# The first FFN of batch 1 beside the attention of batch 0 in a two-FFN transformer layer on one core

## The chip, the core and the metric

The kernel runs on 1 core of one Trainium2 chip. The engines of the core are PE (TensorE, matrix products and transposes), DVE (VectorE), ACT (ScalarE), POOL (GpSimd) and SP (SyncE, which here only issues DMAs). Each runs its own stream of instructions in order; they meet at semaphores. The metric is the time of one execution in microseconds (us), as the median of several.

## What is computed

The reference applies one block to x, 8 batches of 512 rows and 512 columns in f32:

```python
x = x + 0.5 * ffn(layernorm(x))           # gate, up: 512 -> 2048, silu(gate) * up, down: 2048 -> 512
x = x + attn(layernorm(x))                # 16 heads of 32; unit-norm q and k, rope on every other head,
                                          # times q_gain, causal softmax, times w_out
x = x + 0.5 * ffn(layernorm(x))           # the same FFN weights
```

The batches don't depend on each other. Inside a batch the three lines follow one another.

## The kernel before

All weights are loaded once, scaled and split into two f16 parts (high and low) that stay in SBUF. Every product is three f16 matmuls (high x high, high x low, low x high; the helper `three`, L826 to L828), each with its own weight load.

The work of a batch has three parts. I call them FFN1, attention and FFN2.

- An **FFN** takes 32 steps (`STEPS`): 2 halves of 256 rows by 16 chunks of 128 hidden columns. A step, or chunk, is `gate` (12 matmuls of 128x256), `up` (12 more), `gated` (tanh on ACT at L548, two products on DVE at L688 and L690), `parts` (high part on ACT at L553, low part on DVE at L694) and `down` (6 matmuls of 128x512 into PSUM bank 0 and 1, or 6 and 7). After the last down of a half, `residual` (L700 on DVE) adds the sum to x. The downs run two steps behind the gates.
- A **layer norm** has 4 row tiles. For each: `stats` (L661 to L665 on DVE, a power on POOL at L413), `norm` (L675 on DVE), `turn` (4 transposes on PE, L871), `split` (high part on ACT at L495, low part on DVE at L683). In the names (name, u, t) u is the norm: 0 of FFN1, 1 of attention, 2 and 3 of FFN2 (tiles 0 and 1, tiles 2 and 3 of the next passage).
- **Attention** has two halves of 8 heads: `qkv` products (WQ), q and k normalised and rotated (`unit`; L418 and L432 to L437 on POOL), transposed (`stack turn`, L932 and L936), row maxima of the scores (L738 on DVE), scores (L980), `exp` (L533, L537 on ACT, L759 on DVE), `values` (L993, L994), and at the end the product with w_out and `out residual` (L783 on DVE), which writes the result x2 of attention.

Two buffers of 512 x 512 hold x: xa takes the input and FFN1's sum, xb takes x2 and FFN2's sum, and SP stores xb. SP loads the next x into xa when x2 is done.

The order is written out by one function, `order(fill)`, a list of named stages; every engine goes through the same list and runs the stages it has. `stream(fill)` gives the FFN steps in their order, `ffn_units` makes of step j a unit of three pieces (down of step j - 2, gate, up), and inside attention the calls of `some()` put one piece or more between its stages. Pieces left over at the end stand ahead of the product with w_out (`o += sum(pieces, [])`). There are three forms:

- `batch(0, 0, False)`: FFN1 of batch 0, then its attention with nothing in between; the last of the weights are prepared beside its FFN1.
- a loop of B - 1 = 7 passages of `batch(it, 1, True)`: FFN1 of batch it + 1 (behind two steps of FFN2 of batch it), then attention of batch it + 1 with the rest of FFN2 of batch it between its stages.
- `batch(0, B, None)`: FFN2 of batch 7.

Of the kernel before, what the change touches and what calls it, by code (L numbers as in the profile page):

```python
# [49 lines left out]
def build(nc, x, w_qkv, w_out, q_gain, w_gate, w_up, w_down, rope, out):  # L50
# [30 lines left out]
    xb = words("xb").rearrange("p (t d) -> p t d", t=TT)  # L81

# [104 lines left out]
    def per_step(wait, fill):  # L187


        place_of = {fi: j for j, fi in enumerate(stream(fill))}  # L190

        def step(name, f, i, back=0):
            j = place_of[f, i] - back
            if fill is not False:
                wait(name, 2 * STEPS, j + 1 - STEPS)
            elif j >= 0:
                wait(name, 2 * STEPS, j + 1)
        return step

# [28 lines left out]
    def order(fill):  # L228
# [4 lines left out]
        if fill is None:  # L233
# [9 lines left out]
        if fill:  # L243
            (g0, u0), (a0, g1, u1), (d0, g2, u2) = (units.pop(0) for _ in range(3))
            o += [("norm", 3, 2), ("stats", 0, 0)] + g0 + [("turn", 3, 2), ("norm", 3, 3), ("stats", 0, 1), ("split", 3, 2)]
            o += u0 + [("turn", 3, 3), ("norm", 0, 0), ("split", 3, 3)] + a0 + g1
            o += [("turn", 0, 0), ("norm", 0, 1), ("split", 0, 0)] + u1
            o += [("turn", 0, 1)] + d0 + [("split", 0, 1)] + g2 + u2
# [9 lines left out]
        if not fill:  # L258
# [3 lines left out]
        for i in range(STEPS + 2):  # L262
# [13 lines left out]
        for hf in range(2):  # L276
            turns = []
            for t in range(TT + 1):
# [21 lines left out]
                if fill or t == TT:  # L300
                    o += turns
                    turns = []
# [45 lines left out]
    with nc.Block() as block:  # L348

        @block.sync  # L350
        def _(sp):
# [18 lines left out]
            with sp.Fori(0, B - 1) as it:  # L370
                for th in range(2):
                    sp.wait_ge(s["x2_done"], it * TT + 2 * th + 2)
                    sp.dma_start(xa[:, 2 * th:2 * th + 2, :], half_of(x[it + 1], th)).then_inc(s[f"x_in{th}"], 16)
                for th in range(2):
                    sp.wait_ge(s["out_ready"], it * TT + 2 * th + 2)
                    sp.dma_start(half_of(out[it], th), xb[:, 2 * th:2 * th + 2, :]).then_inc(s[f"stored{th}"], 16)
            for th in range(2):
                sp.wait_ge(s["out_ready"], (B - 1) * TT + 2 * th + 2)
                sp.dma_start(half_of(out[B - 1], th), xb[:, 2 * th:2 * th + 2, :]).then_inc(s[f"stored{th}"], 16)
# [4 lines left out]
        def _(pool):  # L384
# [22 lines left out]
            def batch(it, ahead, fill):  # L407
# [3 lines left out]
                def stats(u, t):  # L411
                    wait("var_ready", 12, 4 * u + t + 1)
# [47 lines left out]
            batch(0, 0, False)  # L460
            with pool.Fori(0, B - 1) as it:
                batch(it, 1, True)

        @block.scalar
        def _(act):
# [20 lines left out]
            def batch(it, ahead, fill):  # L486
# [3 lines left out]
                def split(u, t):  # L490
                    if u < 3:
                        wait("xt_ps", 12, 4 * u + t + 1)
                    else:
                        wait("xt_ps", 12, 8 + t + 1, -1)
                    nc.scalar.activation(XT[u // 2][:, 0, :, t * P:(t + 1) * P], ps(turn_bank(u, t)).rearrange("p (k n) -> p k n", k=KC), ACT.Copy).then_inc(s["xt_hi"], 1)  # L495
# [72 lines left out]
            batch(0, 0, False)  # L568
            with act.Fori(0, B - 1) as it:
                batch(it, 1, True)  # L570
            batch(0, B, None)

        @block.vector
        def _(dve):
# [68 lines left out]
            def batch(it, ahead, fill):  # L643
                wait = per(dve, it, ahead)
                step = per_step(wait, fill)
                n = [0]
# [6 lines left out]

                def stats(u, t):
                    src = (xa, xa, xb)[u]
                    if u == 0:
# [6 lines left out]
                    V_.memset(carrier[:, 4 * u + t:4 * u + t + 1], 0.0)  # L663
# [3 lines left out]
                def norm(u, t):  # L667
                    src = (xa, xa, xb, xb)[u]
                    k, batch = (4 * u + t, 0) if u < 3 else (8 + t, -1)
                    wait("rstd_ready", 12, k + 1, batch)  # L670
                    if k >= 2 or fill is not False:
                        wait("xt_ps", 12, k - 1, batch)
# [4 lines left out]
                def split(u, t):  # L677
                    if u < 3:
                        wait("xt_hi", 12, 4 * u + t + 1)
                    else:  # L680
                        wait("xt_hi", 12, 8 + t + 1, -1)
                    c = slice(t * P, (t + 1) * P)
                    V_.tensor_tensor(XT[u // 2][:, 1, :, c], ps(turn_bank(u, t)).rearrange("p (k n) -> p k n", k=KC), XT[u // 2][:, 0, :, c], ALU.subtract).then_inc(s["xt_lo"], 1)  # L683
# [12 lines left out]
                def residual(f, th):  # L696
                    step("down_done", f, HC * (th + 1) - 1)
                    dst, name = ((xa, "x1_done"), (xb, "out_ready"))[f]
                    for t in (2 * th, 2 * th + 1):
                        V_.scalar_tensor_tensor(out=dst[:, t, :], in0=ps(6 * f + t % 2), scalar=unscale[:, 0:1], in1=dst[:, t, :],  # L700
# [78 lines left out]
                def out_residual(_, t):  # L779
                    wait("op_ps", TT, t + 1)  # L780
                    if t % 2 == 0 and fill:
                        wait(f"stored{t // 2}", 16, 16, -1)
                    V_.scalar_tensor_tensor(out=xb[:, t, :], in0=ps(t % 3), scalar=unscale[:, 2:3], in1=xa[:, t, :], op0=ALU.mult, op1=ALU.add).then_inc(s["x2_done"], 1)  # L783
# [29 lines left out]
                assert fill is None or n[0] == LINKS, (n[0], LINKS)  # L813

            batch(0, 0, False)
# [248 lines left out]
```

## Time and profile before

| | us |
|---|---|
| median of 3 runs | 3144.57 |
| lowest, highest | 3142.15, 3144.73 |
| span of the profiled execution | 3141.4 |
| PE busy in it | 2873.6 (91%) |
| DVE busy | 1808.9 (58%) |
| ACT busy | 1225.9 (39%) |
| POOL busy | 401.2 (13%) |

The span runs from the first to the last instruction of the profiled execution; it is 3.2 us shorter than the median of the runs. The page cuts it into 40 slices with a digit for each engine's busy share and one for the clock that TensorE was granted, in tenths of 2.4 GHz. The timeline gives each instruction's start and duration, and in brackets how long its engine had been idle and who ended that. Matmuls overlap in the pipeline, so the pitch from one start to the next, not the duration, is what one costs.

### The profile page before, as it was taken

What the parts mean: (1) busy time and instruction counts of PE and PEld (TensorE: products, weight loads), DVE (VectorE), ACT (ScalarE), POOL (GpSimd) and SP (SyncE); (2) the same over time, 40 slices, a digit from 0 to 9 for tenths busy, and PEclk for the clock granted to TensorE, in tenths of its full rate; (3) what the DMA queues carried; (4) which work ended last, traced back from release to release, by engine and by line L of the source; (5) the groups of instructions that cost most, each with busy time, mean ns of one, the idle gap of its engine ahead of it and who ended that gap; (6) DMA issues with size and microseconds to landing.
All of it is one profiled execution on the core that took longest, in us unless ns stands there. A gap on an engine that the chain in (4) does not pass through costs nothing.

```text
span 3141.4 us, 60646 instructions
## 1 busy us (share of the span) xinstructions
PE 2873.6 (91%) x23744; PEld 2078.2 (66%) x23744; DVE 1808.9 (58%) x4252; ACT 1225.9 (39%) x2218; POOL 401.2 (13%) x438
## 2 busy tenths in 40 slices
PE   4796679999999989999899998999899998999999
PEld 3573357766676667766577666766677665776666
DVE  8645463477535674476634775356744766347743
ACT  5223442355223542255423552235422554235522
POOL 0102200211002200022002110022000220021100
PEclk8896679999999999999999999999999999999999
DMA  6000000000000000000000000000000000000000
GB/s 229 1 1 1 1 14 1 1 8 2 22 1 1 8 22 1 1 2 8 22 1 1 8 2 22 1 1 8 22 1 1 2 8 22 1 1 8 2 8 14
DMA packets 15546, 37.94 MB, mean 12 GB/s; under 512 B 1408, under 2 KB 1408, under 8 KB 14720
## 3 DMA queue, kind: packets, MB, share of 16 engines
q1 hardware_dynamic: 15232, 33.70, 3.0%
q8 instruction: 204, 3.34, 0.4%
q14 instruction: 110, 0.90, 0.1%
HBM read 25.31 MB, written 8.39 MB: 11 GB/s over the span
## 4 chain that ended last, share of the span: by engine, by line
PE 60%; issue 22%; DVE 9%; ACT 5%; POOL 3%; DMA 0%; DVEq 0%; ACTq 0%; POOLq 0%; SPq 0%
PE psum L826 18%; PE psum L827 18%; PE psum L828 18%; ACT arena L537 2%; DVE mneg L738 1%; PE psum L980 1%; ACT arena L533 1%; PE psum L871 1%; PE psum L932 1%; PE psum L936 1%; DVE arena L759 1%; DVE arena L683 1%; POOL rn L418 1%; DVE arena L718 1%; POOL arena L437 1%
## 5 line engine op out<-in xcount | busy, mean ns | idle before, releaser
L826 PE MATMUL psum<-arena,WG 128*128 128x256 f16 x2048 | 564.2, 275 | 25.5 <-issue 19.7
L827 PE MATMUL psum<-arena,WG 128*128 128x256 f16 x2048 | 564.2, 275 | 0.0
L828 PE MATMUL psum<-arena,WG 128*128 128x256 f16 x2048 | 564.1, 275 | 0.0
L826 PE MATMUL psum<-arena,WU 128*128 128x256 f16 x2048 | 561.1, 274 | 0.0
L827 PE MATMUL psum<-arena,WU 128*128 128x256 f16 x2048 | 561.1, 274 | 0.0
L828 PE MATMUL psum<-arena,WU 128*128 128x256 f16 x2048 | 561.0, 274 | 0.0
L688 DVE SCALAR_TENSOR_TENSOR arena<-arena,psum 128x256 f32<-128x256 f32 x512 | 213.7, 417 | 551.9 <-ACT arena L548 551.4
L548 ACT ACTIVATE arena<-psum,tscale 128x256 f32<-128x256 f32 x512 | 242.5, 474 | 670.0 <-PE psum L828 669.4
L826 PE MATMUL psum<-WD,arena 128*128 128x512 f16 x1024 | 389.4, 380 | 34.5 <-DVE arena L694 34.3
L828 PE MATMUL psum<-WD,arena 128*128 128x512 f16 x1024 | 388.6, 379 | 0.0
L827 PE MATMUL psum<-WD,arena 128*128 128x512 f16 x1024 | 388.6, 379 | 0.0
L553 ACT ACTIVATE arena<-arena 128x256 f16<-128x256 f32 x512 | 213.3, 417 | 432.3 <-DVE arena L690 431.5
L694 DVE TENSOR_TENSOR arena<-arena 128x256 f16<-128x256 f32 x512 | 220.2, 430 | 179.9 <-ACT arena L553 179.4
L413 POOL TENSOR_TENSOR rstd<-var,mhalf 128x1 f32<-128x1 f32 x96 | 53.6, 558 | 1783.2 <-DVE var L665 1783.2
L533 ACT ACTIVATE arena<-psum,lnbias,hscale 128x512 f32<-128x512 f32 (+1 forms) x256 | 214.1, 880 | 149.0 <-PE psum L981 148.9
L826 PEld LDWEIGHTS psum<-arena,WG 128*128 128x128 f16 x2048 | 202.0, 99 | 93.0 <-issue 28.3
L418 POOL TENSOR_TENSOR rn<-ss,mhalf 128x16 f32<-128x16 f32 x64 | 186.0, 2906 | 587.5 <-DVE ss L707 586.7
L759 DVE TENSOR_TENSOR arena<-arena 128x512 f16<-128x512 f32 (+1 forms) x256 | 210.9, 824 | 80.8 <-ACT arena L537 77.9
L827 PEld LDWEIGHTS psum<-arena,WG 128*128 128x128 f16 x2048 | 202.2, 99 | 59.7 <-issue 0.3
L690 DVE SCALAR_TENSOR_TENSOR arena<-arena,psum 128x256 f32<-128x256 f32 x512 | 215.3, 420 | 17.6
L738 DVE TENSOR_REDUCE mneg<-psum 128x1 f32<-128x512 f32 (+3 forms) x512 | 214.4, 480 | 11.1 <-PE psum L959 11.1
L828 PEld LDWEIGHTS psum<-arena,WG 128*128 128x128 f16 x2048 | 202.4, 99 | 25.5
(143 smaller groups left out, 4749.5 us busy)
## 6 DMA issues: line engine op xcount, KB each, us to landing
arena<-in_L_attn_x SPq DMA_DIRECT2D x16, 512.0 KB, 3.9
out<-arena SPq DMA_DIRECT2D x16, 512.0 KB, 2.8
arena<-in_L_ffn_w_gate SPq DMA_DIRECT2D x4, 1024.0 KB, 9.2
arena<-in_L_ffn_w_up SPq DMA_DIRECT2D x4, 1024.0 KB, 9.3
WD<-in_L_ffn_w_down SPq DMA_DIRECT2D x4, 1024.0 KB, 11.6
arena<-in_L_attn_w_qkv SPq DMA_DIRECT2D x1, 3072.0 KB, 19.5
WQ<-in_L_attn_w_out SPq DMA_DIRECT2D x1, 1024.0 KB, 21.7
ropet<-rope_table SPq DMA_DIRECT2D x1, 128.0 KB, 2.3
```

What stands on the lines that cost most here:

```text
L418: nc.gpsimd.tensor_tensor(rn[:, c], ss2[:, c], mhalf[:, :], ALU.pow).then_inc(s["r_ready"], 1)
L533: nc.scalar.activation(P32[:, c], ps(0, 0, SW)[:, c], ACT.Exp, bias=lnbias[:, 0:1], scale=hscale[:, k:k + 1])
L548: nc.scalar.activation(fH[i % 2], ps(4 + i % 2, 0, TH), ACT.Tanh, scale=tscale[:, i % HC:i % HC + 1]).then_inc(s["tanh_done"], 1)
L553: nc.scalar.activation(HP[i % 2][0], fH[i % 2], ACT.Copy).then_inc(s["h_hi"], 1)
L688: V_.scalar_tensor_tensor(out=fH[i % 2], in0=fH[i % 2], scalar=1.0, in1=g, op0=ALU.add, op1=ALU.mult).then_inc(s["a_done"], 1)
L690: V_.scalar_tensor_tensor(out=fH[i % 2], in0=fH[i % 2], scalar=2.0 ** -50, in1=u, op0=ALU.mult, op1=ALU.mult).then_inc(s["gated"], 1)
L694: V_.tensor_tensor(HP[i % 2][1], fH[i % 2], HP[i % 2][0], ALU.subtract).then_inc(s["h_lo"], 1)
L738: ins = V_.tensor_reduce(mnegv[:, t, h:h + 1], ps(0, QSEG[t], (t + 1) * P), AX_X, ALU.max, negate=True)
L759: V_.tensor_tensor(PLO[:, c], P32[:, c], PHI[:, c], ALU.subtract).then_inc(s["plo_done"], 1)
L826: T_.matmul(o, lhs(0), rhs(0), start=first, stop=False)
L827: T_.matmul(o, lhs(0), rhs(1), start=False, stop=False)
L828: return T_.matmul(o, lhs(1), rhs(0), start=False, stop=last)
```

## The change

A fourth form takes over. `batch(0, 0, "first")` does FFN1 of batch 0 and then its attention, now with FFN1 of batch 1 between the stages (steps (2, i), residual into xb, layer norm `AHEAD_X` = 4 on 4 tiles, put beside chunks 24 to 32 of FFN1 of batch 0). `batch(0, 1, "second")` does the attention of batch 1 with FFN2 of batch 0 and has no FFN1 of its own. The loop starts with batch 2 and has 6 passages of the old order (its list of stages is unchanged, as is that of "last"). The buffers swap roles: from batch 1 on, the input and FFN1's sum stand in xb, x2 and FFN2's sum in xa; batch 0 keeps xa for all. SP loads x of batch 1 early, behind the end of w_down's preparation and the 4th norm of batch 0. The attention of batch 0 also takes the loop's place for `stack turn` (behind the next qkv).

```diff
+    def x1_of(fill):
+        return xa if fill == "first" else xb
...
+    def norm_of(fill, u, t):
+        if fill == "first":
+            return {0: t, 1: 4 + t if t < 2 else 8 + t, AHEAD_X: 6 + t, 2: 12 + t}[u]
+        if fill == "second":
+            return {3: t, 1: 4 + t, 2: 8 + t}[u]
+        return {3: t - 4, 0: t, 1: 4 + t, 2: 8 + t}[u]
...
     def stream(fill):
-        first = [(0, i) for i in range(STEPS)] if fill is not None else []
-        second = [(1, i) for i in range(STEPS)] if fill is not False else []
-        return second[:AHEAD] + first + second[AHEAD:]
+        first, second, ahead = ([(f, i) for i in range(STEPS)] for f in range(3))
+        if fill == "first":
+            return first + ahead
+        if fill == "loop":
+            return second[:AHEAD] + first + second[AHEAD:]
+        return second
...
-        if fill:
+        if fill != "first":
+            v = 0 if fill == "loop" else 1
             (g0, u0), (a0, g1, u1), (d0, g2, u2) = (units.pop(0) for _ in range(3))
-            o += [("norm", 3, 2), ("stats", 0, 0)] + g0 + [("turn", 3, 2), ("norm", 3, 3), ("stats", 0, 1), ("split", 3, 2)]
+            o += [("norm", 3, 2), ("stats", v, 0)] + g0 + [("turn", 3, 2), ("norm", 3, 3), ("stats", v, 1), ("split", 3, 2)]
...
-        if not fill:
+        if fill == "first":
+            for t in range(TT):
+                for j, name in ((0, "stats"), (1, "norm"), (1, "turn"), (2, "split")):
+                    late.setdefault(HC + 8 + 2 * t + j, []).append((name, AHEAD_X, t))
...
-        for i in range(STEPS + 2):
+        for i in range(STEPS + 2 if fill != "second" else 0):
...
-                if fill or t == TT:
-                    o += turns
-                    turns = []
+                o += turns
+                turns = []
...
+            sp.wait_ge(s["wd_lo"], 4)
+            sp.wait_ge(s["xn_done"], TT)
+            for th in range(2):
+                sp.dma_start(xb[:, 2 * th:2 * th + 2, :], half_of(x[1], th)).then_inc(s[f"x_in{th}"], 16)
+            for th in range(2):
+                sp.wait_ge(s["out_ready"], 2 * th + 2)
+                sp.dma_start(half_of(out[0], th), xa[:, 2 * th:2 * th + 2, :]).then_inc(s[f"stored{th}"], 16)
+            with sp.Fori(0, B - 2) as it:
...
-            batch(0, 0, False)
-            with pe.Fori(0, B - 1) as it:
-                batch(it, 1, True)
-            batch(0, B, None)
+            batch(0, 0, "first")
+            batch(0, 1, "second")
+            with pe.Fori(0, B - 2) as it:
+                batch(it, 2, "loop")
+            batch(0, B, "last")
```

Three places where the streams change. In the rows of after the line numbers are 33 or 34 higher: L721, L723 and L727 are the old L688, L690 and L694.

**PE, where batch 0 goes from FFN1 to its first qkv product (WQ).** Before:

```order
L826 MATMUL psum<-WD,arena 128x512
L827 MATMUL psum<-WD,arena 128x512
L828 MATMUL psum<-WD,arena 128x512
L826 MATMUL psum<-WQ,arena 128x512 [waits pro_lo,sel_done,x1_done,xt_lo]
L827 MATMUL psum<-WQ,arena 128x512
L828 MATMUL psum<-WQ,arena 128x512
```

After:

```order
L860 MATMUL psum<-arena,WU 128x256
L861 MATMUL psum<-arena,WU 128x256
L862 MATMUL psum<-arena,WU 128x256
L860 MATMUL psum<-WQ,arena 128x512 [waits pro_lo,sel_done,x1_done,xt_lo]
L861 MATMUL psum<-WQ,arena 128x512
L862 MATMUL psum<-WQ,arena 128x512
```

The last down of FFN1 (WD) stood right ahead of the qkv product that waits for x1_done; now an up product (WU) of chunk 2 of batch 1 does. In all 3 gate and up products and 1 down of batch 1 stand between the two.

**DVE, in the softmax of the first head group of batch 0.** Before:

```order
L759 TENSOR_TENSOR arena<-arena 128x512 [waits phi_done]
L759 TENSOR_TENSOR arena<-arena 128x768 [waits phi_done]
L738 TENSOR_REDUCE mneg<-psum 128x1 [waits s1_ps] x2
L738 TENSOR_REDUCE mneg<-psum 128x1
L738 TENSOR_REDUCE mneg<-psum 128x1 [waits s1_ps]
L769 RECIPROCAL yrec<-psum 128x4 [waits pv_ps]
L770 COPY arena<-psum 128x4x32
L771 TENSOR_TENSOR arena<-psum,arena 128x4x32 [waits dve_chain]
L773 TENSOR_TENSOR arena<-arena,yrec 128x4x32 [waits y_read]
```

After:

```order
L771 TENSOR_REDUCE mneg<-psum 128x1 [waits s1_ps] x2
L771 TENSOR_REDUCE mneg<-psum 128x1
L771 TENSOR_REDUCE mneg<-psum 128x1 [waits s1_ps]
L721 SCALAR_TENSOR_TENSOR arena<-arena,psum 128x256 [waits tanh_done]
L723 SCALAR_TENSOR_TENSOR arena<-arena,psum 128x256 [waits a_done]
L802 RECIPROCAL yrec<-psum 128x4 [waits pv_ps]
L803 COPY arena<-psum 128x4x32
L804 TENSOR_TENSOR arena<-psum,arena 128x4x32 [waits dve_chain]
L806 TENSOR_TENSOR arena<-arena,yrec 128x4x32 [waits y_read]
L792 TENSOR_TENSOR arena<-arena 128x512 [waits phi_done]
L792 TENSOR_TENSOR arena<-arena 128x768 [waits phi_done]
L727 TENSOR_TENSOR arena<-arena 128x256 [waits h_hi]
```

Between row maxima (L738, now L771), values (L769 on, now L802 on) and low parts of the softmax (L759, now L792) stand the gated products and the low part of an FFN chunk.

**DVE, behind the last out residual of batch 0.** Before (the loop begins; L184 are register instructions that work out semaphore values):

```order
L184 REGISTER_ALU [waits rstd_ready]
L675 TENSOR_SCALAR arena<-arena,mv,rstd 128x512 [waits xt_ps]
L184 ISA
L661 BN_STATS stat<-arena 128x6 [waits x_in0]
L184 ISA
L663 MEMSET carrier 128x1 [waits dve_chain]
L664 BN_AGGR mv<-stat 128x2
L184 REGISTER_ALU
L665 TENSOR_SCALAR var2<-mv 128x1 [waits dve_chain]
L184 REGISTER_ALU
```

After (the straight code of "second"):

```order
L711 TENSOR_SCALAR arena<-arena,mv,rstd 128x512 [waits xt_ps,rstd_ready]
L697 BN_STATS stat<-arena 128x6 [waits x1_done]
L699 MEMSET carrier 128x1 [waits dve_chain]
L700 BN_AGGR mv<-stat 128x2
L701 TENSOR_SCALAR var2<-mv 128x1 [waits dve_chain]
L711 TENSOR_SCALAR arena<-arena,mv,rstd 128x512 [waits xt_ps,rstd_ready]
L697 BN_STATS stat<-arena 128x6 [waits x1_done]
L699 MEMSET carrier 128x1 [waits dve_chain]
L700 BN_AGGR mv<-stat 128x2
L701 TENSOR_SCALAR var2<-mv 128x1 [waits dve_chain]
```

Both go from the last norms of FFN2 (L675, now L711) to new statistics. Before these were of the next input (x_in0) for FFN1; now they are of FFN1's sum (x1_done), for attention.

## Rows read from the trace of the kernel before

**Rows 1.** The page, 40 slices of 78.5 us: PE's busy tenths and its granted clock.

```profile
PE   4796679999999989999899998999899998999999
...
PEclk8896679999999999999999999999999999999999
```

**Rows 2.** Timeline of DVE, columns start us, us, what: first or last L783 of a batch.

```profile
436.41 0.75 DVE L783 SCALAR_TENSOR_TENSOR arena<-psum,unscale,arena 128x512 f32<-128x512 f32 x1 [1.27 <-PE psum L828]
...
442.92 0.74 DVE L783 SCALAR_TENSOR_TENSOR arena<-psum,unscale,arena 128x512 f32<-128x512 f32 x1
...
799.17 0.75 DVE L783 SCALAR_TENSOR_TENSOR arena<-psum,unscale,arena 128x512 f32<-128x512 f32 x1 [1.36 <-PE psum L828]
...
805.68 0.74 DVE L783 SCALAR_TENSOR_TENSOR arena<-psum,unscale,arena 128x512 f32<-128x512 f32 x1
...
2998.39 0.75 DVE L783 SCALAR_TENSOR_TENSOR arena<-psum,unscale,arena 128x512 f32<-128x512 f32 x1 [1.36 <-PE psum L828]
```

**Rows 3.** Stretches: us, then PE, PEld, DVE, ACT, POOL busy, PEclk, DMA share, GB/s.

```profile
93.60:237.10 143.50, 133.02 (x976) 97.59 (x976) 78.76 (x142) 37.73 (x73) 13.48 (x8) 0.96 0.00 1
237.10:443.70 206.60, 133.77 (x992) 79.23 (x992) 112.23 (x267) 89.81 (x131) 43.56 (x44) 0.67 0.01 3
290.00:330.00 40.00, 27.32 (x236) 16.19 (x236) 25.33 (x61) 25.76 (x32) 0.00 (x0) 0.50 0.00 1
443.70:590.80 147.10, 144.97 (x1101) 109.14 (x1101) 63.96 (x158) 35.88 (x79) 4.51 (x8) 0.98 0.02 5
590.80:806.40 215.60, 204.00 (x1846) 144.58 (x1844) 149.33 (x358) 110.20 (x189) 43.65 (x44) 1.00 0.03 9
806.40:957.90 151.50, 146.60 (x1102) 110.07 (x1101) 63.97 (x159) 35.87 (x79) 4.39 (x8) 0.96 0.02 5
```

**Rows 4.** Timeline of PE in the shared stage: units of gate, up, down and turn.

```profile
592.18 0.27 PE L826 MATMUL psum<-arena,WG 128*128 128x256 f16 x1
...
594.80 0.38 PE L826 MATMUL psum<-WQ,arena 128*128 128x512 f16 x1
...
599.14 0.38 PE L826 MATMUL psum<-WD,arena 128*128 128x512 f16 x1
...
600.44 0.60 PE L871 MATMUL psum<-ident,arena 128*128 128x128 f32 x4
...
600.87 0.27 PE L826 MATMUL psum<-arena,WG 128*128 128x256 f16 x1
```

**Rows 5.** Timeline of PE, end of FFN1 of batch 0: idle before, and its releaser.

```profile
234.15 0.39 PE L826 MATMUL psum<-WD,arena 128*128 128x512 f16 x1 [1.09 <-DVE arena L694]
...
237.17 0.38 PE L826 MATMUL psum<-WQ,arena 128*128 128x512 f16 x1 [1.55 <-issue]
```

**Rows 6.** Groups of DVE instructions: busy us, mean ns, idle us before and who ended it.

```profile
L694 DVE TENSOR_TENSOR arena<-arena 128x256 f16<-128x256 f32 x512 | 220.2, 430 | 179.9 <-ACT arena L553 179.4
...
L683 DVE TENSOR_TENSOR arena<-psum,arena 128x512 f16<-128x512 f32 x96 | 66.0, 688 | 40.4 <-ACT arena L495 38.3
L661 DVE BATCH_NORM_STATS2 stat<-arena 128x6 f32<-128x512 f32 x96 | 65.9, 686 | 0.3
...
L675 DVE TENSOR_SCALAR arena<-arena,mv,rstd 128x512 f32<-128x512 f32 x96 | 52.1, 543 | 27.0 <-issue 19.3 <-POOL rstd L413 6.3
...
L664 DVE BATCH_NORM_AGGREGATE mv<-stat 128x2 f32<-128x6 f32 x96 | 17.0, 177 | 4.9 <-issue 1.1
```

**Rows 7.** Timeline of DVE: the fourth norm of batch 0.

```profile
105.10 0.54 DVE L675 TENSOR_SCALAR arena<-arena,mv,rstd 128x512 f32<-128x512 f32 x1
```

**Rows 8.** The page's DMA issues: KB each, median us to landing.

```profile
arena<-in_L_attn_x SPq DMA_DIRECT2D x16, 512.0 KB, 3.9
```

**Rows 9.** Timeline of PE after the attention of batch 0.

```profile
445.19 0.39 PE L826 MATMUL psum<-arena,WG 128*128 128x256 f16 x1 [1.42 <-DVE arena L683]
...
455.17 0.66 PE L871 MATMUL psum<-ident,arena 128*128 128x128 f32 x4 [0.51 <-DVE arena L675]
```

**Rows 10.** Timeline of PE after the first loop-back: the first gate of batch 2.

```profile
810.12 0.39 PE L826 MATMUL psum<-arena,WG 128*128 128x256 f16 x1 [3.13 <-issue]
```

More of the change, by code:

```diff
@@ L190, in per_step, with ffn_norm @@
         place_of = {fi: j for j, fi in enumerate(stream(fill))}
+        late = 0 if fill in ("first", "second") else STEPS
         def step(name, f, i, back=0):
             j = place_of[f, i] - back
[L194 to L197, printed above, removed]
-        return step
+            if fill != "first" or j >= 0:
+                wait(name, 2 * STEPS, j + 1 - late)
+        return step
+    AHEAD_X = 4
+    def norm_of(fill, u, t):
[4 more added lines that the diff above has]
+        return {3: t - 4, 0: t, 1: 4 + t, 2: 8 + t}[u]
+    def ffn_norm(f):
+        return {0: 0, 1: 3, 2: AHEAD_X}[f]
     STEPS = 2 * HC
@@ L566, in batch @@
                      "exp": exp, "y turn": y_turn, "gated": gated, "parts": parts}, fill)
-            batch(0, 0, False)
-            with act.Fori(0, B - 1) as it:
-                batch(it, 1, True)
-            batch(0, B, None)
+            batch(0, 0, "first")
+            batch(0, 1, "second")
+            with act.Fori(0, B - 2) as it:
+                batch(it, 2, "loop")
+            batch(0, B, "last")
         @block.vector
@@ L645, in batch @@
                 step = per_step(wait, fill)
-                n = [0]
+                n = [2 * TT if fill == "second" else 0]
                 def link(ins):
@@ L667, in norm @@
                 def norm(u, t):
[L668 to L672, printed above, removed]
+                    src = normed(u)
+                    k = norm_of(fill, u, t)
+                    wait("rstd_ready", 12, k + 1)
+                    if k >= 2 or fill != "first":
+                        wait("xt_ps", 12, k - 1)
                     if t % 2 and u == 2:
@@ L812, in batch @@
                      "maxima": maxima, "max rows": max_rows, "exp": exp, "y out": y_out, "y turn": y_turn, "out residual": out_residual}, fill)
-                assert fill is None or n[0] == LINKS, (n[0], LINKS)
-            batch(0, 0, False)
-            with dve.Fori(0, B - 1) as it:
-                batch(it, 1, True)
-            batch(0, B, None)
+                assert fill == "last" or n[0] == LINKS + 2 * TT * (fill == "first"), (n[0], LINKS)
+            batch(0, 0, "first")
+            batch(0, 1, "second")
+            with dve.Fori(0, B - 2) as it:
+                batch(it, 2, "loop")
+            batch(0, B, "last")
         @block.tensor
@@ L854, in batch @@
                 step = per_step(wait, fill)
-                bank3 = [("xt_lo", 12, 10, -1) if fill is not False else None]
-                bank2 = [None]
+                bank3 = [("xt_lo", 12, norm_of(fill, 3, 1) + 1) if fill != "first" else None]
+                bank2 = [("x2_done", TT, 3, -1) if fill == "second" else None]
                 scored = [None]
@@ L866, in turn @@
                 def turn(u, t):
-                    k, batch = (4 * u + t, 0) if u < 3 else (8 + t, -1)
-                    wait("xn_done", 12, k + 1, batch)
-                    take(bank3 if turn_bank(u, t) == 3 else bank2, "xt_lo", 12, k + 1, batch)
+                    k = norm_of(fill, u, t)
+                    wait("xn_done", 12, k + 1)
+                    take(bank3 if turn_bank(u, t) == 3 else bank2, "xt_lo", 12, k + 1)
                     for kc in range(KC):
@@ L909, in qkv @@
                         wait("phi_done", 32, 2 * HH)
+                    elif fill == "second":
+                        wait("x2_done", TT, TT, -1)
                     else:
                         wait("x1_done", TT, TT)
-                    if fill is False and i == 0:
+                    if fill == "first" and i == 0:
                         wait("pro_lo", 0, 1 + KC)
@@ L1025, in batch @@
                      "out part": out_part, "out": out_product}, fill)
-            batch(0, 0, False)
-            with pe.Fori(0, B - 1) as it:
-                batch(it, 1, True)
-            batch(0, B, None)
+            batch(0, 0, "first")
+            batch(0, 1, "second")
+            with pe.Fori(0, B - 2) as it:
+                batch(it, 2, "loop")
+            batch(0, B, "last")
 _INS = ["L0_attn_x", "L0_attn_w_qkv", "L0_attn_w_out", "L0_attn_q_gain", "L0_ffn_w_gate", "L0_ffn_w_up", "L0_ffn_w_down"]
```

67 lines of the change are left out of this document (32 added, 35 removed).

## Prediction, written before the changed kernel had run

> **What bounds the kernel now.** I read the page's slices first [rows 1]. PE is 90% busy or more in nearly all of the span; the hole is slices 4 to 6, where both PE's busy share and the granted clock fall to 6 or 7 tenths. The last residual instructions of the attentions, L783 on VectorE (DVE), then cut the span into batches [rows 2]: the one at 442.92 ends the attention of batch 0, the one at 805.68 that of batch 1, and each batch after batch 0 repeats a first FFN and an attention that shares PE with the second FFN of the batch before. Busy time by stage [rows 3] says what limits each:
>
> - attention of batch 0, alone: 206.6 us, of which PE computes 133.8 at a mean granted clock of 0.67. In 290 to 330 us that clock is 0.50, the 1.2 GHz level.
> - attention of batch 1, shared with FFN work: 215.6 us, PE 204.0, clock 1.00. That is 9 us more time, and most of an FFN inside it.
> - first FFN of batch 1: 147.1 us, PE 145.0. Nothing but PE work sets it.
>
> So the shared stages are bound by PE, and the lone attention by its chain through ACT, DVE and POOL. Only this stage has room, and there is one of it. Therefore I build the sum from PE's work plus the few holes in it.
>
> **Prices.** In the shared stage gate and up of one chunk run from 592.18 to 594.80, 2.62 us for 24 matmuls; one down runs from 599.14 to 600.44, 1.30 us for 6; one layer norm turn (4 transposes) from 600.44 to 600.87, 0.43 us [rows 4]. A chunk of FFN thus costs 3.92 us, and 32 of them 125.4 us. All at the 2.4 GHz level.
>
> **The change part by part.** I place each moved piece on the new timeline; t is the start of the first qkv product, as the row at 237.17 now [rows 5].
>
> 1. *End of FFN1 of batch 0.* Ahead of the first qkv product the order puts 3 gate/up and 1 down of batch 1, and 4 more turns: 7.86 + 1.30 + 1.72 = 10.88 us. It takes away two holes of PE, the wait of the last down for L694 (1.09) and the 1.55 us before the first qkv product, which waits for the residual, since other work now stands there [rows 5]. Net 8.2 us: t = 237.2 + 8.2 = 245.4. The 4 norms also add 4 sets of statistics, norm and split on DVE, by the means [rows 6] 0.69 for L661, 0.54 for L675, 0.69 for L683 and three small ones at L664's 0.18 or less, 2.5 us a set at most, and a split and a rstd each on ACT and POOL. One set falls on every second chunk, 7.8 us, where DVE has about 1.3 us per chunk of its own (three like L694's 0.43); I count them at nothing. If that cover were gone it would cost 4 x 2.5 = 10 us.
> 2. *x of batch 1* is now loaded by SP after the 4th norm of batch 0 (L675 at 105.10 [rows 7]) and lands about 3.9 us later [rows 8]; its first reader is chunk 24, near 237 - 9 x 3.92 = 202 us. 90 us of slack, no cost. The stores of batch 0 wait for the same residuals as in the loop now.
> 3. *Attention of batch 0* becomes the shared form. From the first qkv (594.80 [rows 4]) to the end of the last L783 (805.68 + 0.74 = 806.42 [rows 2]) batch 1 takes 211.6 us. Between those points the new order holds the same 27 gates and 28 downs among the attention, and behind its last values product 2 more gate/up and 2 more downs than the loop: 5.24 + 2.60. They stand in a bare FFN tail, whose last down waits as at 234.15, 1.09 us [rows 5]. Total 220.5 us. Batch 0's last L783 ends at 245.4 + 220.5 = 465.9 (now 443.66).
> 4. *Start of batch 1*: no FFN1 any more, only 4 gate/up, 2 downs and 4 turns before its first qkv. From 443.66 to 594.80 there are 151.1 us now, with 37, 35 and 8 of them. Taking 33 x 3.92 + 4 x 0.43 = 131.1 away leaves 20.0 us, which keeps the holes and the half clock behind the last L783 (1.42 and 0.51 us, a first WG matmul of 0.39 us [rows 9] where a warm one takes 0.27 [rows 4]).
> 5. *Attention of batch 1*: 211.6 plus 1 gate/up, 1 down and the 1.09 us tail, 216.6 us. Its last L783 ends at 465.9 + 20.0 + 216.6 = 702.5. Now it is 806.4: **103.9 us gone**.
> 6. *The loop* runs 6 times and no longer 7. The first passage takes 362.76 us (436.41 to 799.17), the later ones (2998.39 - 799.17) / 6 = 366.54 [rows 2]. The difference sits in the start: behind a loop-back PE's first gate idles 3.13 us with "issue" as the reason [rows 10], against 1.42 [rows 9]; the stage with FFN1 takes 151.5 us there, against 147.1 [rows 3]. What is lost is one later passage, with one loop-back: **3.8 us gone**. The last passage and the final FFN stay.
>
> Sum: 103.9 + 3.8 = 107.7 us. The profiled span of 3141.4 becomes 3033.7. The median of the runs, 3144.57, stands 3.2 us above that span, so it becomes **3036.9 us**, a ratio of 0.966.
>
> A shorter way gives the same: the 147.1 + 206.6 us of one FFN1 and the lone attention become one attention stage with its share of chunks.
>
> **Bounds of what the trace does not show.** The new start of batch 1 packs into 20 us four statistics, four norms and four splits (10 us by step 1's set), and about 1.3 us of DVE work for each of 4 chunks: 15 of 20 us, where the same norms had 151 us to settle. The other two norms of this layer follow at once, beside the first qkv. Between nothing (in the loop those two follow at the same place) and their full 5 us on the path, I take nothing: the nearest row is the hole of 0.51 us [rows 9], which the 20 us hold already. On the other side the two tails may find their last part ready (-2.2 us), and the start of batch 1, 5.2 us above its 14.8 us of bare PE work, might lose all of that but the 1.5 us from the last L783 to the first gate (-3.7). So -6 to +5, and a scatter of 2.6 us between the runs of before.
>
> **Rivals.**
>
> *The loop-back is not what makes later passages longer.* Then the first passage is short because a lone attention stands before it, a shared one will stand there now, and the 3.8 us stay: 3040.7. For it: the only short passage is also the only one with that neighbour. Against it: PE's extra hole has "issue" for a reason, no other engine. The Trainium skill (Runtime: NRT & Kernel Launch, Instruction fetch mechanics) states that fetch runs ahead in sequence and that a taken branch out of the window costs a stall. By that rule the 3.8 us go, and by the rival they stay; the row at 810.12 [rows 10] agrees with the rule.
>
> *The low clock belongs to the place, not to idleness (slower).* If PE were granted 0.67 in both new stages as in the lone attention now, 432 us of PE work (204 + 8, and 204 + 16) would take 432 x (1/0.67 - 1) = 213 us more: 3037 + 213 = 3250. It decides from a mean clock of 432 / (432 + 107.7) = 0.80 down. Against it: FFN1 of batch 0 comes earlier and has 0.96, and the shared attention has 1.00 [rows 3]; in the lone one the clock is 0.50 just where PE computes 27 of 40 us. The skill (TensorE: Matmul & The Clock Gate, The HAM clock gate) says that the chip halves this clock when the array has been little busy and gives it back under work; the two stages agree.
>
> *DVE becomes the bound where norms and FFN parts crowd.* The 5 us of the new start or step 1's 10 us, each in full: 3042 to 3047. DVE is 149.3 of 215.6 us busy in the shared stage [rows 3], so waits are short, not absent.
>
> *The hiding doesn't take place.* If x of batch 1 came as late as the last L783 of batch 0, its FFN could not run beside that attention, and 3144 stays. The order and the slack in step 2 speak against it.
>
> **How the numbers follow.** Forecast 3036.9: 0.74. No loop-back gain, 3040.7: 0.10. DVE: 0.08. More gain than the bounds: 0.03. Hiding fails: 0.02. Low clock: 0.03. From the lower bound (-6) to the upper end of the DVE rival and the scatter of before the range is 3031 to 3050. It holds the first three cases; with what may be mis-sized inside the forecast I leave 0.2 outside. Faster by over 0.2% (about what a measurement of this kernel can tell from none): 0.95; within: 0.02; slower: 0.03.
>
> **What would show it.** In the profile of after: no lone attention, granted clock 1.00 from 245 to 466 us; PE busy near 212 us there; the first qkv near 245; the last residual of batch 0's attention ending near 466 and of batch 1's near 702; from the one to the other 237 us; first passage of the loop 363, later ones 366.5. I am wrong if a hole of several us stands before a turn or a gate of the new start (DVE), if the tail of 3 chunks waits more than about 1 us, or if the first passage of the loop takes 366.

## The result and the profile after

| | before | after |
|---|---|---|
| median, us | 3143.36 (3141.70 to 3144.73, 4 runs) | 3031.38 (3028.18 to 3032.48, 4 runs) |
| ratio | | 0.9642, 95% interval 0.9628 to 0.9656 |
| span of the profiled execution | 3141.4 | 3029.8 |

The change takes 112.0 us off; 107.7 were forecast. The mechanism came as predicted, but the saving is 4 to 5 us larger than the forecast, and the time lies at the low edge of the range (3031); a second set of runs (e1, 3030.36) lies below it. So this part is about a small error: which terms of the sum were off, and why the lower bound didn't hold them. One execution of e3, 3199.6 us at a granted clock of 0.912 where the ten others of e3 show 0.957 to 0.959, is left out of its ratio.

In the page's slices after the change, the hole of [rows 1] is gone in both rows:

```profile
PE   4799999999999999998999989999899998999999
...
PEclk8899999999999999999999999999999999999999
```

The stretches of after answer to [rows 3]; the columns are the same. They are FFN1 of batch 0, its attention, the new start of batch 1, its attention, and the first FFN1 of the loop:

```profile
92.35:243.50 151.15, 143.19 (x1070) 106.85 (x1071) 90.81 (x176) 41.46 (x81) 15.95 (x13) 0.96 0.02 8
243.50:464.00 220.50, 207.87 (x1876) 147.22 (x1874) 149.42 (x357) 111.42 (x191) 43.63 (x44) 1.00 0.01 1
464.00:482.90 18.90, 16.88 (x125) 13.07 (x125) 13.70 (x39) 5.44 (x11) 3.01 (x5) 0.91 0.00 1
482.90:699.30 216.40, 203.78 (x1846) 144.32 (x1844) 147.86 (x354) 110.43 (x189) 43.62 (x44) 1.00 0.03 9
699.30:845.80 146.50, 143.83 (x1102) 108.50 (x1101) 64.02 (x159) 35.89 (x79) 4.50 (x8) 0.99 0.02 5
```

The attention of batch 0 now holds 208 us of PE work at a granted clock of 1.00, where it held 133.8 at 0.67. In the new start DVE is busy 13.7 of 18.9 us, and PE 16.9. PE's two idle times there are the 1.50 us before its first gate, shown below, and 0.51 us before a turn, the same as in [rows 9]:

```profile
474.60 0.66 PE L905 MATMUL psum<-ident,arena 128*128 128x128 f32 x4 [0.51 <-DVE arena L711]
```

So no queue of norms on DVE holds PE up. The last out residual of each batch (L816, the old L783) answers to [rows 2]. These are batches 0, 1, 2 and 7:

```profile
463.22 0.74 DVE L816 SCALAR_TENSOR_TENSOR arena<-psum,unscale,arena 128x512 f32<-128x512 f32 x1
...
698.57 0.74 DVE L816 SCALAR_TENSOR_TENSOR arena<-psum,unscale,arena 128x512 f32<-128x512 f32 x1
...
1060.68 0.74 DVE L816 SCALAR_TENSOR_TENSOR arena<-psum,unscale,arena 128x512 f32<-128x512 f32 x1
...
2892.40 0.74 DVE L816 SCALAR_TENSOR_TENSOR arena<-psum,unscale,arena 128x512 f32<-128x512 f32 x1
```

The sum laid beside two executions of the changed kernel (the second is the profile of run e1, below) shows where it was short. A stage ends with the last out residual of its batch, or begins with PE's first gate or first qkv product:

| stage, us | forecast | first profile | e1 |
|---|---|---|---|
| up to the first gate | 93.6 | 92.4 | 93.6 |
| FFN1 of batch 0 | 151.8 | 151.2 | 149.7 |
| attention of batch 0 | 220.5 | 220.4 | 220.4 |
| start of batch 1 | 20.0 | 19.0 | 18.7 |
| attention of batch 1 | 216.6 | 216.4 | 216.4 |
| first passage of the loop | 362.8 | 362.1 | 362.0 |
| five later passages | 1832.7 | 1831.7 | 1830.9 |
| rest, FFN2 of batch 7 | 135.8 | 136.7 | 136.9 |
| span | 3033.7 | 3029.8 | 3028.6 |

The two attentions, which are dense PE work at 2.4 GHz and short holes, agree within 0.2 us. All that differs by more lies where the clock changes, or ahead of the first gate, where the weights are prepared. PE behind the attention of batch 0 shows what I had not priced. This is the timeline at the start of batch 1, the answer to [rows 9]:

```profile
465.57 0.27 PE L860 MATMUL psum<-arena,WG 128*128 128x256 f16 x1 [1.50 <-DVE arena L716]
...
466.49 0.42 PE L860 MATMUL psum<-arena,WG 128*128 128x256 f16 x1
...
469.45 0.27 PE L860 MATMUL psum<-arena,WU 128*128 128x256 f16 x1
```

A 128x256 matmul of 0.42 us is one at 1.2 GHz, of 0.27 one at 2.4. The low stretch begins after the first gate has started and ends before 469.45, some 3.4 us. In the kernel before it began with the first gate, at 445.19, and lasted 5.3 us. I measured this stretch behind every attention, from the start of the first slow 128x256 matmul to that of the last: 2.3 to 9.2 us in both kernels, and not the same at the same place of two executions of one kernel.

### The profile page after: what moved, and what is told of

Its sections match the earlier page's. It is cut to its first block, busy times and chain, and to the rows that moved or that the text cites. A ratio compares the mean times of both kernels' runs of the same rounds, so it can differ in the third digit from the quotient of the medians.

```text
span 3029.8 us, 60069 instructions
## 1 busy us (share of the span) xinstructions
PE 2831.6 (93%) x23744; PEld 2061.9 (68%) x23744; DVE 1807.5 (60%) x4252; ACT 1221.4 (40%) x2218; POOL 402.4 (13%) x438
## 4 chain that ended last, share of the span: by engine, by line
PE 60%; issue 20%; DVE 10%; ACT 6%; POOL 3%; DMA 0%; DVEq 0%; ACTq 0%; POOLq 0%; SPq 0%
PE psum L860 18%; PE psum L862 18%; PE psum L861 18%; ACT arena L567 3%; DVE mneg L771 1%; PE psum L905 1%; DVE arena L792 1%; ACT arena L563 1%; PE psum L968 1%; PE psum L972 1%; PE psum L1016 1%; POOL rn L450 1%; DVE arena L727 1%; DVE arena L716 1%; POOL arena L469 1%
## 5 line engine op out<-in xcount | busy, mean ns | idle before, releaser
L721 DVE SCALAR_TENSOR_TENSOR arena<-arena,psum 128x256 f32<-128x256 f32 x512 | 214.0, 418 | 492.8 <-ACT arena L578 492.3
L727 DVE TENSOR_TENSOR arena<-arena 128x256 f16<-128x256 f32 x512 | 220.6, 431 | 169.6 <-ACT arena L583 169.1
L792 DVE TENSOR_TENSOR arena<-arena 128x512 f16<-128x512 f32 (+1 forms) x256 | 211.2, 825 | 84.3 <-ACT arena L567 82.9
L723 DVE SCALAR_TENSOR_TENSOR arena<-arena,psum 128x256 f32<-128x256 f32 x512 | 215.4, 421 | 17.6
L771 DVE TENSOR_REDUCE mneg<-psum 128x1 f32<-128x512 f32 (+3 forms) x512 | 215.0, 483 | 10.6 <-PE psum L995 10.6
```

The lines of the kernel that those rows point to most:

```text
L721: V_.scalar_tensor_tensor(out=fH[i % 2], in0=fH[i % 2], scalar=1.0, in1=g, op0=ALU.add, op1=ALU.mult).then_inc(s["a_done"], 1)
L723: V_.scalar_tensor_tensor(out=fH[i % 2], in0=fH[i % 2], scalar=2.0 ** -50, in1=u, op0=ALU.mult, op1=ALU.mult).then_inc(s["gated"], 1)
L727: V_.tensor_tensor(HP[i % 2][1], fH[i % 2], HP[i % 2][0], ALU.subtract).then_inc(s["h_lo"], 1)
L771: ins = V_.tensor_reduce(mnegv[:, t, h:h + 1], ps(0, QSEG[t], (t + 1) * P), AX_X, ALU.max, negate=True)
L792: V_.tensor_tensor(PLO[:, c], P32[:, c], PHI[:, c], ALU.subtract).then_inc(s["plo_done"], 1)
```

## The experiments

The times are medians, and the interval behind each ratio is the 95% one. Ratios are to the kernel before, whose runs on the same chip gave 3143.31 for e1 to e4, 3144.24 for e5 to e8 and 3145.29 for e9 to e11.

**e1: the changed kernel again.** 

> The changed kernel once more, to see how much of the 5.5 us by which it beat the forecast (3031.4 against 3036.9) repeats, and in which stage. Theory A (sizes): the saving is 110 to 114 us again, and the stages stand as in the first profile: first qkv 151.2 us behind the first gate, attention of batch 0 220.4, start of batch 1 about 19. Theory B (scatter): the saving varies by 2 us or more from chip to chip and run to run, and the first gate's start (92.35 in the first profile, 93.64 in the kernel before) and the stretches of low clock behind each attention move by about 1 us each.

3030.36 us, ratio 0.9639 (0.9626 to 0.9652): 113.0 us less than before. The saving repeats; it isn't a lucky run. Its stages are in the table: the two attentions and the start of batch 1 agree with the first profile within 0.3 us. FFN1 of batch 0 doesn't (149.7 against 151.2; I had expected 151.2), and the first gate began at 93.58, not 92.35. The trace shows why FFN1 differs: its first matmuls run at 1.2 GHz, 14 of them of 128x256 in e1 and 23 in the first profile, and 5 and 10 more follow behind a hole of 6.53 us near 147 us. A slow one is 0.21 us behind the one before it, a fast one 0.11, so 14 slow ones less are the 1.5 us. Both theories hold in part: about 5 us over the forecast are real, 1 to 2 us in several stages are scatter. The runs of e1 to e11 also show how a span stands to its own run: about 2.0 us below it for the kernel before (1.7 to 2.1), 1.75 for the changed one. I had taken 3.2, by pairing a span with the median of other runs. Some 1.4 us of the forecast time was that.

**e2: one passage outside the loop.**

```diff
-            with pe.Fori(0, B - 1) as it:
-                batch(it, 1, True)
+            batch(0, 1, True)
+            with pe.Fori(0, B - 2) as it:
+                batch(it, 2, True)
```

(the same on the other engines). 

> The kernel before with the first passage of its loop written straight behind batch 0, so that the loop runs 6 times; the list of stages is unchanged. Theory A (a taken branch costs the start of a passage): one loop-back less, 3140 - 3.8 = about 3.8 us faster than before, ratio 0.9988; both straight passages are short ones, the passage behind the peeled one (batch 2) also 362 to 363 us. Theory B (the lone attention in front makes the first passage short): no gain, ratio 1.000, and the passage of batch 2 takes 366.5.

3137.39 us, ratio 0.9983 (0.9974 to 0.9992), 5.9 us faster; by the interval 2.5 to 8.2 us, so it shows that a loop-back costs something, not whether it is 3.8 us. The passages of batches 1 and 2 take 361.5 and 363.6 us, the five behind them 365.4 in the mean. The second of the short ones has a shared attention in front of it, so the rival "no loop-back gain" falls. In this profile the lone attention took 211.0 us and not 206.5, at a clock of 0.66: with a low clock for most of its length, that stage scatters by more than the whole effect sought.

**e3: only the place of the stack turns.**

```diff
-                if fill or t == TT:
-                    o += turns
-                    turns = []
+                o += turns
+                turns = []
```

> The kernel before with only the changed place of the stack turns in the attention of batch 0 (behind the next qkv product). Theory A: this part of the change is worth little by itself, within 0.3% (10 us) either way, since the lone attention waits on its chain ACT, DVE, POOL. I take -5 to 0 us, as the four holes of 6.1 us ahead of the last two turns of each half might shrink. Theory B: it is a large part of the gain, 20 us or more.

3144.47 us, ratio 1.0003 (0.9994 to 1.0012). This part of the change shows no worth of its own, in the kernel where the attention stands alone; the interval leaves room for 2 us of gain or 4 of loss. I had left it unpriced, and that was right.

**e4: all of the change but the hiding.**

```diff
-                if len(pieces) > 1:
+                if len(pieces) > 1 and fill != "first":
```

> The changed kernel with the pieces of the first FFN of batch 1 all put behind the attention of batch 0 and none between its stages. Same work, same buffers, same loads. Theory A (the gain is the room under the lone attention): nearly all of it goes, 245 + 206 for the lone attention, 120 for the FFN behind it, 20 and 217 for batch 1, one loop-back less: 3138 to 3146 us, with the granted clock of the attention near 0.67 again. Theory B (the gain comes from the other parts, the swapped buffers, the early load, the straight code): it keeps half of the gain or more, below 3090 us.

3131.4 us, ratio 0.9964 (0.9950 to 0.9978). Of 112 us 12 are left, and 100 are gone: the gain is the work laid into the room of the lone attention. The new kernel's attention of batch 0 and the FFN behind it, as stretches:

```profile
239.50:446.00 206.50, 139.86 (x1050) 83.92 (x1049) 110.88 (x263) 92.28 (x137) 42.68 (x42) 0.68 0.00 1
446.00:565.50 119.50, 116.13 (x857) 83.82 (x856) 44.04 (x102) 25.27 (x56) 1.12 (x2) 1.00 0.00 1
```

From the first qkv product to the last out residual it takes 326.0 us, the 206 + 120 that I had. The cut at 446.00 is placed by that sum; FFN pieces begin at 431.80 already, ahead of the product with w_out, and up to there the mean clock is 0.65, behind it 1.00. The whole came out 7 us below the low end of what I expected: 5.5 us of that is the first qkv product, at 239.5 and not at 245, since the edit also moves a chunk (3.92 us) from ahead of it to behind the attention. 3.8 us of the 12 were expected as the lost loop-back. By the traces, the two batches up to 801.50 end 4.9 us earlier than before, and the six passages behind them take 6.6 us less than the last six in the kernel before. The first of them has no loop-back in front of it; the later five take 365.8 in the mean instead of 366.4, though no work differs in those. That was the first sign that the passages themselves scatter.

**e5: the six passages written out straight.**

```diff
-            with pe.Fori(0, B - 2) as it:
+            for it in range(B - 2):
                 batch(it, 2, "loop")
```

> The changed kernel with its 6 passages written out straight, no loop on the four computing engines (SP keeps its own). Theory A (the taken branch costs): 5 loop-backs less, each 3.8 to 4.2 us: 19 to 21 us faster than the changed kernel, about 3011 us; each passage takes 362 to 363 us. Theory B (the branch costs nothing, or straight code has to be fetched at the same price): within 3 us of the changed kernel, passages of 366.

3008.07 us, ratio 0.9563 (0.9550 to 0.9576), 23 us less than the changed kernel. Three rows of DVE give the passages, those of batches 2, 3 and 7:

```profile
1061.42 0.74 DVE L816 SCALAR_TENSOR_TENSOR arena<-psum,unscale,arena 128x512 f32<-128x512 f32 x1
1423.17 0.74 DVE L816 SCALAR_TENSOR_TENSOR arena<-psum,unscale,arena 128x512 f32<-128x512 f32 x1
...
2870.43 0.74 DVE L816 SCALAR_TENSOR_TENSOR arena<-psum,unscale,arena 128x512 f32<-128x512 f32 x1
```

361.75 us for the first, (2870.43 - 1423.17) / 4 = 361.8 for the rest. Against 366.3 a loop-back costs 4.5 us, not 3.8. Of these 4.5 us 0.3 lie in the attention, which takes 211.3 us in the straight form and 211.6 in the loop; the rest lies in the start of the passage.

**e6: two passages in each turn of the loop** (3 turns, the passages' order unchanged). 

> The changed kernel with two passages in each turn of the loop, 3 turns: 2 loop-backs, not 5. Theory A: 3 x 4 = 12 us faster than the changed kernel, about 3020 us, and passages alternate between 362 and 366. Theory B: within 3 us of it.

3021.93 us, ratio 0.9603 (0.9590 to 0.9617). 9.5 us less for three loop-backs, where 12 were expected and e5 would give 13.5. Passages behind a loop-back take 365.2 and 367.0, the others 362.5 to 363.5: these are longer than the 361.8 of e5, with low stretches of 4.5 to 6.8 us in front of them instead of 3.3 to 3.8.

**e7: the last down's wait covered.**

```diff
-        o += sum(pieces, [])
-        o += [("out part", 0, 1), ("y turn", 1, 1), ...
+        rest = sum(pieces, [])
+        at = max(k for k, x in enumerate(rest) if x[0] == "down")
+        o += rest[:at] + [("out part", 0, 1)] + rest[at:]
+        o += [("y turn", 1, 1), ...
```

> The changed kernel with the first out part of row tile 1 (9 matmuls, about 1.9 us) put ahead of the last down wherever leftover pieces stand behind the attention. It should cover the wait of 1.09 us of the last down in batches 0 and 1; in the loop this down had no such wait. Theory A: about 2.2 us faster than the changed kernel, 3029. Theory B (the wait only moves to the y turn or the product with w_out behind it): no change.

3026.39 us, ratio 0.9623 (0.9610 to 0.9636), 4 to 6 us less and not 2.2. The hole in the changed kernel is this row of PE, 1.09 us as [rows 5] let expect:

```profile
450.23 0.39 PE L860 MATMUL psum<-WD,arena 128*128 128x512 f16 x1 [1.09 <-DVE arena L727]
```

Here the attentions of batches 0 and 1 take 219.1 and 215.1 us, 1.3 less each: 2.6 us. The attentions in the loop take 211.4 us instead of 211.6, some 1.5 us in six. The rest lies in the starts of the passages: the later ones take 365.4 us instead of 366.3, and in the profile three of five have a low stretch of only 2.3 us. e10 tests whether that is a gain or luck.

**e8: PE kept busy in the lone attention of the kernel before.**

```diff
+                def warm(f, i):
+                    for kc in range(KC):
+                        three(ps(4 + i % 2, 0, TH), lambda q: WG[:, q, kc, 0:P],
+                              lambda q: WU[:, q, kc, 0:TH], kc == 0, kc == KC - 1)
```

at every second call of `some()`. 

> The kernel before with 43 groups of 12 matmuls of 128x256 added on PE alone in the attention of batch 0 (two ahead of its first qkv, the others between its stages), into a PSUM bank that nobody reads there; nothing is left out. They are 56 us of PE work at 2.4 GHz. Theory A (the low clock of that attention is the price of an idle PE): the granted clock rises from 0.67 to 0.9 or more, the attention's own matmuls shrink to full-clock durations, and the stage still takes 198 to 214 us. Theory B (the low clock belongs to this place of the program): it stays near 0.67, the added work takes 84 us or more and the stage 240 us or more.

3136.65 us, ratio 0.9973 (0.9962 to 0.9983): 56 us of work more, 7 us of time less. The stretch of that attention:

```profile
237.70:438.20 200.50, 159.82 (x1486) 113.91 (x1484) 112.06 (x264) 88.45 (x131) 43.63 (x44) 0.95 0.01 4
```

The clock rises from 0.67 to 0.95 at the same place of the program, with the same ACT, DVE and POOL work, and the stage takes 200.5 us, not 206.6 (nor 208.6 and 211.0 as in e3 and e2). So the low clock follows PE's idleness, not the place; the slow rival is refuted. It also splits the cost of the lone attention: the chain through ACT, DVE and POOL needs 200 us at most by itself (the added matmuls may hold it up here and there), and the low clock added 6 or more.

**e9: the holes behind every attention filled.** The same group of matmuls, in the changed kernel, twice at the end of each attention:

```diff
-              ("out", 0, 3), ("turn", 2, 1), ("out residual", 0, 3),
+              ("out", 0, 3), ("warm", 0, 0), ("turn", 2, 1), ("warm", 0, 1), ("out residual", 0, 3),
```

> The changed kernel with two groups of 12 matmuls of 128x256 on PE alone at the end of every attention, one ahead of the last turn and one behind it, into a PSUM bank nobody reads there; nothing is left out. They stand in PE's two holes of 2.27 and 1.4 to 1.5 us. Theory A (the stretch of 1.2 GHz behind each attention, 2.5 to 9.4 us long, is the price of these holes, and its changing length is what makes the passages differ by 2 us): the stretches vanish or shrink, every passage loses 1 to 4 us, 8 to 20 us in all, and the passages agree within 0.5 us. Theory B (the stretch has another cause, or the loop-back alone keeps it): passages stay at 365 to 367 or grow by the 0.3 to 2.6 us of added work that the holes don't take.

3023.56 us, ratio 0.9619 (0.9606 to 0.9632): 6 to 8 us less, with 8 x 2.6 us more PE work. PE at the start of batch 1:

```profile
464.58 0.63 PE L905 MATMUL psum<-ident,arena 128*128 128x128 f32 x4 [0.96 <-DVE arena L716]
465.05 0.27 PE L860 MATMUL psum<-WU,WG 128*128 128x256 f16 x1
...
466.71 0.27 PE L860 MATMUL psum<-arena,WG 128*128 128x256 f16 x1 [0.20 <-DVE arena L716]
```

Of the holes of 2.27 and 1.50 us, 0.96 and 0.20 are left; the first gate stands as far behind the attention as without the added matmuls (1.62 us), and every 128x256 matmul stays at 0.27. No low stretch is left but one, of 3.2 us, behind the first loop-back, where PE still idles:

```profile
1066.98 0.28 PE L860 MATMUL psum<-arena,WG 128*128 128x256 f16 x1 [3.59 <-issue]
```

The five later passages now agree: 364.6 to 365.2 us, where the changed kernel had 365.5 to 367.2. So most of the scatter of the passages was the length of the low stretch. What is left of the cost of a loop-back is 3.1 us: the first passage, with no loop-back in front of it, takes 361.9 us and the later ones 365.0. At the other four loop-backs PE idles 1.9 to 3.4 us before the first gate, without a low stretch behind.

**e10: straight and with the covered wait.** 

> The changed kernel with its 6 passages written out straight and the first out part of row tile 1 ahead of the last down of each attention. Theory A (the two savings add): 23 us of the straight form and 3 to 5 us of the covered wait, 3003 us against 3031, passages of 361. Theory B (the covered wait was worth 5 us only by a luckier low clock behind the loop-backs): 3005 to 3008 us.

3007.36 us, ratio 0.9562 (0.9549 to 0.9576), the same as e5 within the intervals. The attentions of batches 0 and 1 keep their 1.3 us each, but the low stretches behind the attentions are now 3.4 to 5.7 us long instead of 3.3 to 3.8, and the passages take 362.1 us instead of 361.8. So the clock takes the gain back, as in Theory B. That is more than luck in one execution: the mean granted clock is 0.982 to 0.983 in all five runs here and 0.985 to 0.986 in all five of e5 (on another chip; the kernel before has 0.957 to 0.959 on both). Of the 4 to 6 us of e7, 4.1 lie in its attentions; whether the rest was a luckier clock is not shown: its five runs have 0.979 to 0.981, those of the changed kernel 0.980 to 0.982.

**e11: e10 and the filled holes.** 

> The same with the two groups of 12 matmuls of the filled holes at the end of every attention. Theory A (holes cost clock): low stretches of 3.4 us, half of it lost, go away, about 1.7 us in each of 8 starts, 10 to 14 us less than without them: 2990 to 2994 us. Theory B: no gain or a loss of up to 2.6 us for each attention, 3003 to 3023 us.

3000.03 us, ratio 0.9539 (0.9526 to 0.9552). 7.3 us less than e10; I had expected 10 to 14, so the mechanism is right and 1.7 us for a start was too much: it is 0.9. The trace shows where part of it goes. With the clock held, PE reaches the turns of the start earlier and waits longer for the norms on DVE (L713 here), 0.93 and 0.78 us, where e10 has one such wait of 0.51:

```profile
1423.23 0.66 PE L907 MATMUL psum<-ident,arena 128*128 128x128 f32 x4 [0.93 <-DVE arena L713]
```

DVE's rows (L818 here) for batches 3 and 7:

```profile
1418.47 0.74 DVE L818 SCALAR_TENSOR_TENSOR arena<-psum,unscale,arena 128x512 f32<-128x512 f32 x1
...
2863.10 0.74 DVE L818 SCALAR_TENSOR_TENSOR arena<-psum,unscale,arena 128x512 f32<-128x512 f32 x1
```

(2863.10 - 1418.47) / 4 = 361.16, and all six passages are equal to 0.05 us; no low stretch stands behind any attention. It is faster than both kernels, by 145 us (the kernel before, on the same chip) and some 31 (the changed one). A variant with real FFN work in the holes, instead of matmuls that nobody reads, was not tried.

## Why the mechanism was right and the size fell short

What failed are terms of the sum, and then its lower bound. Steps 4 and 6 priced stages with a stretch of low clock in them from one execution as if that length were fixed: the start of batch 1 at 20.0 us, measured 19.0 and 18.7, and the loop's first passage at 362.76, measured 362.1. The step from the span to the median (3.2 us, measured 1.75) and the time up to the first gate (93.6, measured 92.4 and 93.6) were taken from one execution too. The 5.5 us between 3036.9 and 3031.4 add up so, by the first profile: 1.2 start-up, 0.6 FFN1 of batch 0, 1.0 start of batch 1, 0.3 the two attentions, 1.7 the passages, less 0.9 for the last FFN, which came out longer; then 1.4 for the step to the median, and the profiled run lies 0.2 above the median.

- **The bound, and the room in one stage**: right. e4 takes the hiding away and 100 of 112 us with it; e3 shows no worth of the new place of the turns.
- **Steps 3 and 5**, the shared attentions: right to 0.2 us, with the same wait of 1.09 us in front of the last down. Counting PE's instructions at their pitch works where PE is dense and its clock constant. The sign "PE busy near 212 us" was wrong by 4 us: the 204.0 of [rows 3] is counted from 590.8, 4 us ahead of the first qkv product, and the stage holds 207.9. The "shorter way" named under the sum is not worked out there and confirms nothing.
- **Step 1**: right within 0.6 us in the first profile and 2 us in e1. The four extra norms on DVE cost nothing that is seen. Step 2, the early load, too: x of batch 1 is issued at 104.33 us, and no wait for it is seen.
- **Step 4 was mis-sized**, 20.0 against 19.0 and 18.7. I had kept "the holes and the half clock" of the one start that the trace showed in that form. Its low stretch was 5.3 us long, the new ones 3.4 and 2.3. At half speed about half of the difference is time lost.
- **Step 6 was mis-sized** in the same way. The first passage of the kernel before has that 5.3 us stretch inside, so 362.76 was no clean price: 361.8 is (e5), and a loop-back costs 4.5 us, not 3.8. By the first profile that is 0.65 us on the first passage and 1.0 on the later five.
- **The last FFN** erred the other way. Taken over unchanged at 135.8 us, it took 136.7 and 136.9, behind low stretches of 4.4 and 4.9 us where the kernel before had 3.2. That part of the errors cancels is luck.
- **The base**: 1.4 us from pairing a span with the median of other runs, and 1.2 us of start-up in the first profile, none in e1: the first gate comes at 92.1 to 94.5 us over all these profiles, whatever the kernel.
- **The bounds** failed with these terms. I built the low end from holes that might close (-6) and took 2.6 us of scatter on the high end only. Eight starts, each with a low stretch of 2.3 to 9.2 us, were in the sum as one draw each. Their own scatter, some 1 us a passage, and the error of the base belonged at both ends; with what is known now, 3027 to 3050 would have held all runs.
- **The rivals**: the low clock as a property of the place is refuted by e8, and by the 1.00 of both new attentions; DVE as the bound by the 0.51 us above, the only wait of PE for a norm in the new start; the missing loop-back gain by e2 and e5; the failed hiding by the result.

## What to carry to other kernels

A stage that runs alone on its latency chain (each engine waiting for the one before), in a kernel whose other stages are bound by PE, is room for PE work. Here it took in most of an FFN for 14 us more of its own time (206.5 to 220.4), and the gain could be priced by counting at PE's pitch. Before a passage is taken as a unit price, split its holes from the clock behind them: take several executions or several passages, and give the term the spread that they show, at both ends. Where a loop turns only a few times over a long body, compare it with the body written out: here each loop-back cost 4.5 us.

## What the runs showed of the hardware that I had not expected

- **More work, less time.** 43 groups of matmuls that nobody reads made the lone attention 6 us shorter (e8), and two groups behind each attention took 7 us off the kernel (e9, and again in e11 against e10), because PE kept its 2.4 GHz level.
- **Short holes were enough to lose the clock.** Idle times of 2.3 and 1.5 us, with one turn of 0.6 us between them, brought a stretch of 1.2 GHz each time; 0.96 and 0.20 us brought none. Behind filled holes, one idle time of 3.59 us at a loop-back brought a stretch and one of 3.38 us at another did not (e9). The stretch lasted 2.3 to 9.4 us over all profiles and differed between executions. The Trainium skill (TensorE: Matmul & The Clock Gate, The HAM clock gate) says that the number of slow matmuls varies from run to run and is not to be fitted; these traces agree.
- **A loop-back** leaves PE idle for 2.6 to 3.8 us before its first gate, with no other engine to wait for, against 1.4 to 1.5 in straight code. With the clock nearly held, a passage behind it is 3.1 us longer than one of the same execution without it (e9), and 3.8 us longer than in e11, where the covered down wait and the straight code are in the figure too.
- **The clock at the start has the same scatter.** FFN1 of batch 0 took 149.7 us in e1 with 19 slow 128x256 matmuls, 150.2 in e9 with 24, and 151.2 to 151.5 in the other executions of the changed forms with 33 to 37 (e4, whose edit moves a chunk out of it, aside).
- What stays open: why the low stretch has its various lengths.
